# Which steps' drives GpSimd makes: rows 1, 2, 6, 7, 13, 14 in place of 1, 3, 6, 8, 11, 14

## The reference

```
u      = silu(conv(in_proj(ctx)) + bias)            # (b, DI, L)
x_dbl  = x_proj(u); dt, B, C = split(x_dbl)         # B, C: 16 rows of length L per batch
delta  = softplus(dt_proj(dt) + dt_bias)            # (b, DI, L)
for every channel and each of 16 states n, along the sequence l:
    state_n[l] = state_n[l-1] * exp(delta[l] * A_n) + (delta[l] * u[l]) * B_n[l]
y[l]   = sum over n of state_n[l] * C_n[l] + D * u[l]
x      = x + swap(y * silu(layernorm(x)))
x      = x + dense(layernorm(x)) + experts(layernorm(x))
```

## Time and profile before

| what | value |
| --- | --- |
| median of 3 runs | 2089.46 us (2079.15 to 2089.96) |
| the profiled execution | 2086.44 us |
| its span in the trace | 2084.7 us |
| what lies around the span | 1.7 us |
| granted TensorE clock, mean | 0.917 of full |
| VectorE busy | 1789.8 us, 86% |
| GpSimd busy | 1768.5 us, 85% |
| TensorE busy | 1768.3 us, 85% |
| ScalarE busy | 1259.4 us, 60% |

### The profile page before, as it was taken

How to read it: one execution, slowest core, us unless ns; L and a number is a source line. 1 busy time by engine, 2 the same in 40 slices (tenths; PEclk the granted TensorE clock), 3 DMA queues, 4 the chain that set the end, 5 groups by cost and what they waited for, 6 DMA issues and landing times.

```text
span 2084.7 us, 23748 instructions
## 1 busy us (share of the span) xinstructions
PE 1768.3 (85%) x7996; PEld 1086.3 (52%) x7996; DVE 1789.8 (86%) x1435; ACT 1259.4 (60%) x1704; POOL 1768.5 (85%) x796
## 2 busy tenths in 40 slices
PE   8777778776789889898999889888888888888999
PEld 3344444454555555555555555555555555554554
DVE  3699999999899999998999999998989999996111
ACT  3465656555566766766666766666666666663331
POOL 0399999999999999999999999999999999997200
PEclk9878787778779999999999999999999999999999
DMA  4658655586756566687666656686766656565200
GB/s 154 241 185 280 205 194 183 200 277 250 249 199 208 198 215 223 223 301 286 231 223 209 210 192 213 222 286 245 241 203 220 211 201 211 200 214 219 79 31 31
DMA packets 158985, 435.88 MB, mean 209 GB/s; under 512 B 14640, under 2 KB 47664, under 8 KB 158864
## 3 DMA queue, kind: packets, MB, share of 16 engines
q1 hardware_dynamic: 158864, 434.37, 60.5%
HBM read 383.46 MB, written 50.86 MB: 208 GB/s over the span
## 4 chain that ended last, share of the span: by engine, by line
DVE 39%; PE 29%; issue 16%; ACT 6%; POOL 5%; DMA 4%; DVEq 0%; SPq 0%; POOLq 0%; ACTq 0%
DVE state L1124 24%; DVE row L1109 11%; PE bank_a L550 8%; PE y_ps L494 5%; POOL prod L1265 4%; DVE conv L1101 3%; PE bank_b L550 3%; PE row L572 2%; DMA xrow<-in_x 2%; PE row L488 2%; ACT decay L844 2%; PE bank_a L561 2%; PE bank_b L454 1%; PE bank_b L445 1%; ACT L708 1%
## 5 line engine op out<-in xcount | busy, mean ns | idle before, releaser
L1265 POOL TENSOR_TENSOR prod<-state,c_rows 128x1024 f32<-128x1024 f32 x512 | 1201.2, 2363 | 75.6 <-DVE state L1124 38.2
L1124 DVE TENSOR_TENSOR_SCAN state<-decay,row 128x1024 f32<-128x1024 f32 x334 | 763.0, 2284 | 7.4
L494 PEld LDWEIGHTS y_ps<-ident,prod 128*128 128x128 f32 x4096 | 516.0, 151 | 286.7 <-issue 186.2
L494 PE MATMUL y_ps<-ident,prod 128*128 128x128 f32 x4096 | 587.1, 291 | 37.8 <-POOL prod L1265 35.0
L1109 DVE TENSOR_TENSOR row<-du,row 128x1024 f32<-128x1024 f32 x334 | 404.4, 1211 | 34.4 <-PE row L488 33.9
L1258 POOL TENSOR_TENSOR drive_rows<-du,b_rows 128x1024 f32<-128x1024 f32 x178 | 421.6, 2368 | 5.4 <-DMA b_rows<-bc_d 5.4
L844 ACT ACTIVATE row<-delta,a 128x1024 f32<-128x1024 f32 x178 | 199.2, 1119 | 373.6 <-DVE state L1124 373.1
L550 PE MATMUL bank_a<-w_o,xnT 128*128 128x512 f32 x816 | 399.7, 621 | 18.2 <-DVE x L1171 18.0
L1124 DVE TENSOR_TENSOR_SCAN state<-row,drive_rows 128x1024 f32<-128x1024 f32 x178 | 404.8, 2274 | 9.6 <-POOL drive_rows L1258 8.3
L844 ACT ACTIVATE decay<-delta,a 128x1024 f32<-128x1024 f32 x334 | 374.7, 1137 | 0.0
L488 PE MATMUL row<-parts,sel 96*128 96x512 bf16 x668 | 221.1, 415 | 180.2 <-DVE state L1124 174.0
(11 more groups left out here) (138 smaller groups left out, 1639.2 us busy)
## 6 DMA issues: line engine op xcount, KB each, us to landing
c_rows<-bc_d SPq DMA_DIRECT2D x512, 512.0 KB, 4.4
xrow<-in_x SPq DMA_DIRECT2D x32, 512.0 KB, 7.1
skip<-u_d SPq DMA_DIRECT2D x32, 512.0 KB, 6.2
yy_d<-yy SPq DMA_DIRECT2D x32, 512.0 KB, 6.3
b_rows<-bc_d SPq DMA_DIRECT2D x24, 512.0 KB, 8.0
u_d<-conv SPq DMA_DIRECT2D x24, 512.0 KB, 5.4
ctx<-u_d SPq DMA_DIRECT2D x48, 256.0 KB, 6.0
x<-in_x SPq DMA_DIRECT2D x24, 512.0 KB, 5.7
```

What stands on the lines that cost most here:

```text
L494: last = nc.tensor.matmul(y_ps[:, i * P:(i + 1) * P], source[:, i * P:(i + 1) * P], ident[:, :], start=(first and i % (H // P) == 0), stop ...
L1124: nc.vector.tensor_tensor_scan(state[:, q % STATES, :], factor, term, 0.0, ALU.mult, ALU.add).then_inc(scan_done, 1)
L1265: nc.gpsimd.tensor_tensor(prod[:, q % PRODS, :], state[:, q % STATES, :], c_rows[:, q % RING, :], ALU.mult).then_inc(prod_ready, 1)
```

## The change

One tuple of row numbers moves, and with it the condition that turns one of its members into a D step where a block has no halves (8 before, 7 now). There are as many P steps as before, 178 in all, and as many D steps, 334.

```diff
-B_ROWS = (1, 3, 6, 8, 11, 14)
-ON_POOL = [tuple(n for n in B_ROWS if n != 8 or len(HALVES[E]) > 1) for E in range(NBLK)]
+B_ROWS = (1, 2, 6, 7, 13, 14)
+ON_POOL = [tuple(n for n in B_ROWS if n != 7 or len(HALVES[E]) > 1) for E in range(NBLK)]
```

## The result

| | before | changed |
| --- | --- | --- |
| median, device us | 2087.05 (4 runs, 2079.15 to 2089.96) | 2194.62 (4 runs, 2193.14 to 2198.27) |
| ratio | | 1.0524 (95%: 1.0491 to 1.0558) |
| profiled execution | 2086.44 | 2195.09 |
| its span | 2084.7 | 2193.3 |
| mean granted TensorE clock | 0.917 | 0.888 |

The changed kernel is 5.2% slower, 108.6 us by the two spans. The forecast was slower, 2167 us with a range of 2120 to 2200. The direction and the range held, the latter by 5 us; of the 108 us it had 80.

What follows compares the result with a forecast made beforehand. A nearly full VectorE and GpSimd loop was taken to bound the blocks. Early 24.5, middle 35, late 14 and three leftover periods 7 made 80.5 us on 2086.4: 2167 us, range 2120 to 2200.

Steps and rivals of the forecast that it cites:

- The loop: VectorE leads from gated_y to scan 10, GpSimd from product 10 to 15; 53.5 of a 55.0 us period, 1.5 slack.
- (a): GpSimd, products 10 to 15: row 13's drive now stands ahead of product 11, ten operations for nine, +2.32 us.
- (c): Within GpSimd's leg: drive 14 ends 10.7 us after scan 10, wanted at 9.7, so scan 14 waits about 1.0.
- (b): VectorE, gated_y to scan 10: step 2's multiply, hidden ahead of gated_y, becomes step 3's behind it, +1.24 us.
- the multiply alone: Rival: GpSimd has slack and take_v is not late, so 31 x 1.24 = 38 us, time 2125; chance 0.16.
- (d): take_v behind two decays delays y to 7.05 us after scan 0; early blocks with three halves lose 3.5 us.
- (e): Middle blocks, 9 to 22: period 58.2 us grows by 2.5, with bounds of +1.24 and +3.5.
- clock rival: Rival: TensorE's clock falls in middle and late blocks too, 103 us slower, time 2189; chance 0.18.
- Late blocks: Blocks 24 to 31: the loop grows from 55.0 to 57.0 us, +2.0 a period, seven periods making 14 us.
- (f): Priced at nothing: decays of steps 2, 7, 14 (at most 28 us), experts' wait gone, b_rows loads, untouched dense tail.
- nothing: Rival: the 1.5 us of slack a block and VectorE's waits absorb everything, time 2086; chance 0.03.
- faster: Rival: ScalarE's loads run ahead, TensorE spreads rows in time, 33.9 us of spread waits go, time 2053; chance 0.03.

Runs made afterwards that it cites:

- last pair alone: Kernel before with only the last P step pair moved, tuple (1, 3, 6, 8, 13, 14): 2136.65 us, ratio 1.0239.
- take_v first: Changed kernel with ScalarE's first take_v moved ahead of the decays in section 1: 2166.74 us; the same edit on the first pair alone: 2092.21 us.
- first pair: Kernel before with only the first P step pair moved, tuple (1, 2, 6, 8, 11, 14): 2151.06 us, ratio 1.0304.
- drive 13 early: Changed kernel with GpSimd's drive of row 13 issued ahead of product 9 in place of product 11: 2173.88 us; with take_v first besides: 2117.46 us.
- the leg and take_v repaired: Changed kernel with the drive of row 13 ahead of product 9 and take_v ahead of the decays in section 1: 2117.46 us, ratio 1.0124.
- three repairs: Changed kernel with drive 13 ahead of product 9, take_v first and VectorE's residual half ahead of scan 12 in place of 13: 2094.49 us, ratio 1.0037.
- early drive 14: Kernel before with GpSimd's drive of row 14 issued ahead of product 10 in place of product 12: 2079.71 us, ratio 0.9951.
- the last run: Changed tuple with drives 13 and 14 ahead of products 9 and 10, take_v first, residual half ahead of scan 12, gated_y at step 3: 2102.93 us, ratio 1.0072.

## Why the prediction was right, and where it was mis-sized

**The loop and its direction.** Right. GpSimd's waits for scans grew by 105.5 us (I had 60 to 100, so a little low), all at or ahead of product 10, VectorE's waits at gated_y to 95.5 (70 to 110), with no busy time added to either.

**(a) GpSimd's leg, +2.32, and (c), the wait of scan 14.** Right in place, a little low in size. The last pair alone costs 48 us (I had at most 45), scan 14 waits in all 31 blocks, 28.1 us (I had 20 to 40). In a late block it waits 1.00 as worked out:

```profile
1836.24 2.29 DVE L1124 TENSOR_TENSOR_SCAN state<-row,drive_rows 128x1024 f32<-128x1024 f32 x1 [1.00 <-POOL drive_rows L1258]
```

**(b) The multiply behind gated_y, +1.24 a block.** Right where the loop is closed; alone it was not measured. With take_v first, late blocks have a period of 57.4 with both pairs (57.0 was worked out) and 56.0 with the last pair alone, 1.4 for what the first pair adds. Without the longer leg and with take_v first, the first pair costs 4 us over all blocks, where my rival of the multiply alone had 38. The slack of the loop may take in part of it. Part is a gain that the prediction did not have: TensorE no longer spreads row 2 ahead of dt_half, and y comes 1.36 us earlier in block 4.

**(d) take_v.** Right, and the largest single cause: putting take_v first takes 59 us of the first pair's 62 back (2151.06 to 2092.21). y came 6.9 after scan 0 against 7.05 worked out (its sum has a slip of 0.1: the four terms before dt_half make 2.8 and not 2.9), take_v 2.2 after it against 2.3. Early blocks lost 3.2 a period, 3.5 forecast. Their waits at gated_y were to be 4.5 to 5 each; they are 4.3 to 4.5 in blocks 1, 2, 4 and 5, and 2.9 in blocks 3, 6 and 8, where product 15 ends only 4.1 to 4.5 after scan 0 and GpSimd's leg decides.

**(e) Middle blocks, 2.5 forecast, 4.0 measured.** The step that failed in size. I took the chain to y at full clock, 5.2 after scan 0. In block 18 it took 6.9, as in an early block: TensorE paused for take_v, and dt_half behind the pause ran at the lower clock. 14 periods by 1.5 make 21 of the 28 us that the forecast lacked. The longer chain accounts for a part of them: over the 14 blocks the wait at gated_y is 3.0 on average in place of 2.4, which is 9 us. Where the other 12 lie was not worked out. Nor is take_v's pause the only one: with take_v first the transposes in block 18 ran at the lower clock as well, behind a wait for product 15. From 600 to 1450 us the granted clock is 0.92 with take_v first, and 0.96 with drive 13 early besides, as in the kernel before: the longer leg has its part in the clock too.

My clock rival had this (3.5 a middle period), and the measured 2195 is nearer to its 2189 than to my 2167. I had it as a clock that falls over whole stages, to be read from the slices of the page; what happened is short, in the 4 us behind a pause, inside blocks that run at full clock else. The Trainium skill, TensorE: Matmul & The Clock Gate, Part 1, says that activity releases the throttled state. The trace agrees, with 0.50 behind a pause of 3.29 us. The profile's row of slices, against the earlier trace rows, shows a 9 turned 8 here and there:

```profile
PEclk9877788777879999899999999899988898899999
```

**Late blocks, 2.0 forecast, 3.0 measured.** Here too the lower clock stands behind a pause. TensorE paused 0.98 us for take_v, and product 15's transposes took 1.97 in place of the 1.09 of the earlier trace rows:

```profile
1849.15 1.43 PE L454 MATMUL bank_b<-xd,w_bdt 32*128 32x512 f32 x2 [0.98 <-ACT delta L755]
1850.51 1.97 PE L494 MATMUL y_ps<-ident,prod 128*128 128x128 f32 x8
```

That is 0.9, about the 1.0 a period that is missing. But the pause for take_v does not explain the clock by itself. In the first pair alone TensorE pauses for take_v just as long in block 28, and dt_half and the transposes stay at full clock:

```profile
1756.15 1.12 PE L454 MATMUL bank_b<-xd,w_bdt 32*128 32x512 f32 x2 [0.98 <-ACT delta L755]
1757.20 1.09 PE L494 MATMUL y_ps<-ident,prod 128*128 128x128 f32 x8
```

What the changed kernel has besides is a longer wait for the residual add earlier in the block, 2.9 us a late block on average against 0.7. Whether that is what lowers the clock at the transposes was not separated.

**(f) At nothing.** The decays inside the pairs were covered but for 10.1 us in 5 waits, within the 28 that I had allowed. What I had missed altogether is the residual: I wrote that the gates come earlier and the wait behind them can go. They did, and TensorE's wait for the gates fell (24.8 to 10.3 us), only for TensorE to wait for VectorE's residual add instead, 48.5 us in place of 18.0. I take it that in the changed kernel this lies largely beside GpSimd's leg, which no run shows; with the leg and take_v repaired it was worth 23 us.

**The other rivals.** The multiply alone, nothing and faster were all excluded by the interval. After three repairs the whole of the change but 6 us is gone (2094.49), so take_v's place, GpSimd's order and the residual's place carry nearly all of it. take_v first and the residual's earlier half were not tried on the kernel before, which may gain from them as well, as it gained 9 us from an early drive 14. So the 6 us are not the price of the tuple alone. The three are things that the tuple moved other work against; that a pair can cost by itself too is what the last run shows.

## What to carry to other kernels

When two engines are each nearly full and wait a little for each other, look for the loop between them and count what stands on each leg; an operation moved from outside the leg into it can cost up to its full length in every round, though no engine does more. Moving a step also moves what is queued behind it: the most expensive effect here was that of a 0.67 us ScalarE operation that slid behind two others it has nothing to do with. It can also take work out of a chain, as the spread of row 2 here, and that has to be counted too. Single repairs of such a loop understate: 28 and 21 us alone were 77 together.

## What was not expected of the hardware

TensorE's clock can fall behind pauses within a block. After a wait of 3.29 us the granted clock was 0.50 for the next 4 us, and after one of 3.88 six matmuls took 5.49 us in place of 2.74. That was among the worst of its kind: behind the 14 such waits of that run, 2.7 to 3.9 us long, the six matmuls took from 2.84 to 5.49. So a wait of TensorE can be paid for twice: as itself, and in the work behind it. The wait's length alone does not tell: 1.81 us went with a fall in block 18 of one kernel, 0.98 with a fall in the changed kernel and with none in the first pair alone. A long stretch hides all this: from 600 to 1450 us the changed kernel's granted clock is 0.92 as a whole (0.96 before).

```profile
600.00:1450.00 850.00, 731.92 (x3355) 459.61 (x3356) 763.46 (x618) 536.05 (x732) 761.11 (x341) 0.92 0.62 209
```
